# A two-layer gated cross-attention and routed-expert block on one core: the context's load goes to ScalarE's queue, and the load of x's first batch to SyncE's queue behind the key weight

## The reference

```python
q = (query @ Wq.T).reshape(B, L, H, D) * scale      # query: layer-normed x, 4 x 512 x 256
k = (key @ Wk.T).reshape(B, -1, H, D)               # key, value: the context, 4 x 64 x 256
v = (value @ Wv.T).reshape(B, -1, H, D)
scores = jax.nn.sigmoid(jnp.einsum('blhd,bshd->bhls', q, k))
o = jnp.einsum('bhls,bshd->blhd', scores, v).reshape(B, L, E)
return o @ Wo.T
...
h = jax.nn.gelu(jnp.einsum('th,ehf->tef', x_flat, W1) + b1[None], approximate=False)
y = jnp.einsum('tef,efh->teh', h, W2) + b2[None]
```

## Time and profile before

| | before |
|---|---|
| median of 3 runs | 707.21 us (706.15 to 713.72) |
| the profiled execution's own time | 707.39 us |
| its span, first to last instruction | 705.2 us |
| TensorE busy | 670.1 us, 95% |
| VectorE busy | 475.9 us, 67% |
| ScalarE busy | 466.1 us, 66% |
| GpSimd busy | 300.9 us, 43% |
| mean granted TensorE clock over the span | 0.988 |

### The profile page before, as it was taken

How to read it: one execution, slowest core, us unless ns; L and a number is a source line. 1 busy time by engine, 2 the same in 40 slices (tenths; PEclk the granted TensorE clock), 3 DMA queues, 4 the chain that set the end, 5 groups by cost and what they waited for, 6 DMA issues and landing times.

```text
span 705.2 us, 21900 instructions
## 1 busy us (share of the span) xinstructions
PE 670.1 (95%) x7546; PEld 569.8 (81%) x7547; DVE 475.9 (67%) x1184; ACT 466.1 (66%) x1182; POOL 300.9 (43%) x221
## 2 busy tenths in 40 slices
PE   7998999999999999999999989998999999999992
PEld 4543767688788899989899979766999999999992
DVE  5899787858778676666654569985995554544541
ACT  3585887655399787877766547933997566566560
POOL 1101353444626565555545233402465555555432
PEclk9999999999999999999999999999999999999997
DMA  9972010337079857899876479964544444544432
GB/s 286 375 275 73 9 32 31 91 71 261 26 242 250 176 118 158 213 225 246 200 161 117 67 219 416 370 219 121 146 81 67 78 80 75 90 67 76 77 50 23
DMA packets 110680, 104.98 MB, mean 149 GB/s; under 512 B 53067, under 2 KB 96085, under 8 KB 109734
## 3 DMA queue, kind: packets, MB, share of 16 engines
q1 hardware_dynamic: 95126, 83.27, 39.1%
q0 software_dynamic: 14976, 20.58, 18.5%
q10 hardware_dynamic: 528, 0.52, 0.2%
HBM read 64.84 MB, written 28.23 MB: 132 GB/s over the span
## 4 chain that ended last, share of the span: by engine, by line
PE 70%; DVE 11%; DMA 6%; ACT 4%; issue 4%; POOL 2%; SPq 1%; POOLq 0%; DVEq 0%; ACTq 0%
PE bank L1285 9%; PE bank L1283 9%; PE bank L1284 9%; PE bank L1296 9%; PE bank L1298 8%; PE bank L1297 8%; PE bank L1408 2%; DMA x_arena<-token_rows,gather_now 2%; PE bank L966 2%; DVE weights L1867 1%; PE bank L1018 1%; DMA x_arena<-x_arena 1%; DVE work L1887 1%; PE bank L1020 1%; PE bank L1019 1%
## 5 line engine op out<-in xcount | busy, mean ns | idle before, releaser
L1638 ACT ACTIVATE work<-bank,b_cols 128x128 f32<-128x128 f32 x624 | 176.3, 384 | 136.1 <-PE bank L1285 127.8
L1283 PE MATMUL bank<-x_arena,weights 128*128 128x128 f16 x1248 | 213.2, 219 | 3.1 <-DMA x_arena<-x_arena 1.6
L1285 PE MATMUL bank<-x_arena,weights 128*128 128x128 f16 x1248 | 213.2, 219 | 0.0
L1284 PE MATMUL bank<-x_arena,weights 128*128 128x128 f16 x1248 | 213.2, 219 | 0.0
L2134 DVE TENSOR_TENSOR work<-work 128x512 f16<-128x512 f32 x156 | 100.9, 688 | 115.1 <-ACT work L1646 110.2
L1296 PE MATMUL bank<-weights,work 128*128 x624 | 170.2, 273 | 2.5 <-issue 1.3
L1298 PE MATMUL bank<-weights,work 128*128 x624 | 170.1, 273 | 0.0
L1297 PE MATMUL bank<-weights,work 128*128 x624 | 170.1, 273 | 0.0
L849 POOL DMA_INDIRECT x_arena<-token_rows,gather_now x78 | 85.0, 1089 | 139.2 <-DVE gather_now L2128 95.6
L1283 PEld LDWEIGHTS bank<-x_arena,weights 128*128 x1248 | 122.1, 98 | 6.3 <-issue 2.9
L1284 PEld LDWEIGHTS bank<-x_arena,weights 128*128 x1248 | 122.1, 98 | 0.8
(11 more groups left out here) (251 smaller groups left out, 1212.9 us busy)
## 6 DMA issues: line engine op xcount, KB each, us to landing
weights<-in_L_ffn_W SPq DMA_DIRECT2D x76, 256.0 KB, 7.3
raw<-in_L_ffn_W SPq DMA_DIRECT2D x44, 256.0 KB
split_dram<-row_arena SPq DMA_DIRECT2D x12, 512.0 KB
weights<-split_dram SPq DMA_DIRECT2D x3, 2048.0 KB, 16.9
odd_sum<-padding_row SPq DMA_DIRECT2D x1, 2176.0 KB, 13.4
token_rows<-row_arena SPq DMA_DIRECT2D x1, 2072.0 KB, 6.7
weights<-in_L_ffn_sW SPq DMA_DIRECT2D x8, 256.0 KB, 7.3
x_sum<-x_arena SPq DMA_DIRECT2D x4, 512.0 KB, 3.4
```

What stands on the lines that cost most here:

```text
L1283: nc.tensor.matmul(o, w1_at[f][c][0].block(), hi, start=c == 0, stop=False)
L1284: nc.tensor.matmul(o, w1_at[f][c][0].block(), lo, start=False, stop=False)
L1285: m = nc.tensor.matmul(o, w1_at[f][c][1].block(), hi, start=False, stop=c == DC - 1)
L1638: m = nc.scalar.activation(hid[:, k, f * P:f * P + P], h_ps[k][half][:, g * P:g * P + P], ACT.Gelu, bias=b1_cols[n][:, f, bass.ds(e, 1)], ...
```

## The change

The load of the context is taken from SyncE's queue and becomes ScalarE's only load, in the place of x's first batch. The load of that batch goes to SyncE's queue, behind the key weight and ahead of the query weight. The semaphores and the waits of all engines stay as they are.

```diff
         def _(sp):
             sp.dma_start(const_sb[:, :], const[:, EARLY:]).then_inc(in_const, 16)
-            sp.dma_start(ctx_in[:, :, :], a["ctx_1024"].rearrange("b s d -> (b s) d").rearrange("(t p) d -> p t d", p=P)).then_inc(in_ctx, 16)
             def load_w(w, ready):
                 sp.dma_start(w_in[:, w, :, :], attend0_src(w).rearrange("(c p) i -> p c i", p=P)).then_inc(ready, 16)
 
             def load_x(b):
                 sp.dma_start(x_sb[:, TB * b:TB * b + TB, :], batch_of(x_rows, b)).then_inc(in_x[b], 16)
 
-            for w in (1, 0, 2, 3):
+            load_w(1, in_w[1])
+            load_x(0)
+            for w in (0, 2, 3):
                 load_w(w, in_w[w])
...
         def _(act):
-            act.dma_start(x_sb[:, 0:TB, :], batch_of(x_rows, 0)).then_inc(in_x[0], 16)
+            act.dma_start(ctx_in[:, :, :], a["ctx_1024"].rearrange("b s d -> (b s) d").rearrange("(t p) d -> p t d", p=P)).then_inc(in_ctx, 16)
             act.wait_ge(consts_ready, 5)
```

## The result

The changed kernel is slower by a small, clear amount. Its median is 712.06 us over 20 runs (708.53 to 720.33), that of before in the same rounds 707.92 us over 20 runs (705.35 to 713.72). The ratio is 1.0047, with a 95% interval of 1.0026 to 1.0068, which is 3.3 us, between 1.8 and 4.8 (the run of 720.33 us was a slow one and is left out of the ratio; the two medians stand 4.1 us apart, within that interval). This is within 1%, as forecast, but the median lies above the range of 706.4 to 710.0 us. The profiled execution took 708.92 us, beside 707.39 of before.

What follows compares the result with a forecast made beforehand. The start was taken as bound by bytes, with the chain waiting for the context's landing at 6.05 us. The profiled 707.39 plus 0.75 us, clock cost unchanged, gave 708.1 us, 708.0 as a median; range 706.4 to 710.0 us.

Steps and rivals of the forecast that it cites:

- The margin of 0.76 us and VectorE's order: Before the key product, VectorE's context copy had 0.76 us to spare over ScalarE's weight copy, but follows x's statistics.
- The landings: First loads, by bytes ahead: context about 4.6 us, key weight 5.3, x 6.85, query weight 7.55 as before.
- the term of 0.75 us: Key product's first load starts at 9.56 instead of 8.81 us, behind VectorE's copy: 0.75 us later.
- The clock: TensorE's clock at the start: its cost was kept as before, with the key product at 2.13 us.
- the two gaps: New TensorE waits before the key product, for the query weight and for VectorE: 0.8 and 0.9 us.
- The rival with the price of 1.4 us more: TensorE's clock stays low through the key product, 3.5 instead of 2.13 us; 709.5 us in all; chance 0.25.
- The shift goes to the end whole: From the key product to the kernel's end, no wait swallows the delay of 0.75 us.
- the clock rival: Low TensorE clock through the key product: a shift of 2.15 us, 709.5 us in all; chance 0.25.
- the transposes behind it: Twelve transposes after the key product, also at the low clock: shift 3.5 us, 710.9 us in all; chance 0.05.
- The two terms: The key product's later start, forecast 0.75 us, and TensorE's clock, whose cost was kept as before.
- Faster: Key product starts earlier if x lands before 6.09 us; at most 0.45 us gained, 706.9 us; chance 0.07.
- nothing moves: At the start, loads don't reorder as counted or the margin takes x's delay; 707.4 us; chance 0.1.

Runs made afterwards that it cites:

- the context behind x: Kernel before with only the context's load moved to ScalarE's queue, behind x's first batch; ratio 1.0013 (0.9984 to 1.0043).
- The products of ones: Changed kernel with products of ones, results unused, in TensorE's three gaps at the start; key product 1.80 us, ratio 1.0015 (0.9981 to 1.0049).
- the kernel with the delay: Kernel before with 44 unused products of ones between the key product's waits and the key product; ratio 1.0153 (1.0111 to 1.0195).
- x alone moved: Kernel before with only x's first batch moved, to SyncE's queue behind the key weight; context stays on SyncE's queue; ratio 1.0033 (1.0002 to 1.0064).

## Why the prediction was wrong, and where it was right

- *The margin of 0.76 us and VectorE's order.* Right. The key product waited for VectorE's copy, at 10.14 and 9.42 us, and came earlier when the copy was taken ahead of the statistics.
- *The landings.* Context and key weight came as counted (4.47 and 5.2 us; 4.6 and 5.3 predicted). x was taken at 6.85 us with bounds of 6.24 and 7.34; it came at 7.35 and 6.63 us in two profiles. So the term of 0.75 us measured 1.33 and 0.68 us, 1.0 in the mean. The byte count behind it came out near for this kernel, but does not hold as a rule over two queues, as the context behind x showed.
- *The clock.* This is the step that failed. "I keep the clock's cost as before: work begins 1.45 us earlier, and the two gaps take 1.7 us out of it" put the key product at 2.13 us. It took 3.3 and 3.5 us. The rival with the price of 1.4 us more was the right one, and had 0.25. The extra cost measured 1.2 us against before's first profile and 0.9 us between the means. The products of ones, which gave 1.5 us and more back, show that it is the clock. The first gap was also longer than counted, 1.62 us against 0.8, since in the changed kernel the key weight's turn ended at 6.54 and the query weight landed at 8.11, not 7.55 us; the second, 0.87 us, was as counted (0.9). In the second profile they were 1.40 and 0.45 us. That these two gaps, and nothing else in the earlier start, keep the clock low isn't shown by itself: the kernels that have one or both of them, without products of ones, took 3.3 to 3.55 us for the key product, but those that have neither took 2.1 to 3.2 us.
- *A second fault in the same term.* I read the clock's course in one profile, low until 9.4 us, as a property of the kernel before. In its second profile, with the same work on TensorE, the clock was up first, fell at about 7.7 us and rose again at about 11.1 us. That moved the first query product by 0.7 us, a third of the 2.1 us that the change costs there, and one profile can't tell of it.
- *The shift goes to the end whole.* Right as far as the runs tell: 10.1 us at the start gave 10.8 us (7.9 to 13.8). In the single pairs of profiles it didn't stay whole (2.48 us became 1.7, and 1.7 became almost nothing). For 1.2 to 1.3 us in each pair this went with a fall of TensorE's clock near 460 us that only before's execution had. The sum has no such term; it is scatter between executions.
- *The range.* 710.0 us as upper end took the clock rival without the transposes behind it, and a spread of runs from three of them. The median of before itself moved from 707.21 to 707.92 with 20 runs. The two terms as measured, 2.1 us, give 710.0 us on that median. The rest up to 712.06, or up to the ratio's 3.3 us, is within the interval (2.1 lies between 1.8 and 4.8), and no trace locates it: both pairs of profiles are less than 2.1 us apart at the end. It stays open.
- *Faster, or nothing moves.* Neither came; x was never near 6.1 us.

## What to carry to other kernels

Before a load is moved forward, ask which engine consumes it and what that engine waits for first in its fixed order: here the earlier context lay in the bank until VectorE had received x. Waits in TensorE's start can cost twice, once in the wait and once in a clock that stays low; filling the idle time with unused products ahead of the waits was worth more at the start (0.9 to 1.5 us earlier) than any order of the loads, though the kernel's time could not be told from no change. And where a term of a microsecond decides, take two profiles of the same kernel: two of before differed by 0.7 us at the first query product, and a difference at the start is read there, not at the end of a pair of profiles.

## What was not expected of the hardware

- The course of TensorE's clock differs between executions of the same work: low until 9.4 us in before's first profile; up at 6.4 us, low from 7.7 to 11.1 us and up again in the second; low until 11.5 us in the kernel with the delay, whose start is the same. With unbroken products from 0.98 us, the transposes at 4.34 us were fast already. With a gap of 0.39 us among the products, they were all slow until 6.9 us; yet with x alone moved, a gap of 0.47 us was followed by a rise at 4.8 us, and in before's second profile the clock was up behind 2.68 us of idling. So no rule on gaps comes out of these traces. The Trainium skill (TensorE: Matmul & The Clock Gate, "What's actually happening") says that the number of slow products varies from run to run of the same kernel. These traces agree; I had weighed the page's other sentence only.
- In the two kernels in which ScalarE issued no load, the constants landed 2.2 and 2.3 us after their issue, in all others 2.8 to 3.3 us. Whether the second issuer or the shared engines make the difference wasn't tried.
- The traffic can fall to 202 GB/s for a microsecond in one execution of a kernel and stay at 344 GB/s in the next, and with it x's landing moves by 0.7 us. Its cause is open.
